# Two graph-attention layers and a mixture of experts on one core: attention on all context rows, its result gathered onto x by accumulating DMAs

## What is computed

```python
def gat_layer(x, adj, W, a_self, a_neigh, b):
    feat = jnp.einsum('nf,hfo->hno', x, W)
    e = leaky_relu(attn_self[:, :, None] + attn_neigh[:, None, :])
    e = e + MASK_VAL * (1.0 - adj)[None, :, :]
    alpha = jax.nn.softmax(e, axis=-1)
    out = jnp.einsum('hnm,hmo->hno', alpha, feat) + b[:, None, :]
    return jax.nn.elu(out reshaped to [n, 512])

h = gat_layer(ctx, a, W0, ...);  attn = gat_layer(h, a, W1, ...)   # ctx [4,512,128], a = layernorm(x)
x = x + attn                                                      # x [4,512,512]
x = x + moe(layernorm(x))       # 32 experts, top 4 of 3 groups, capacity 80, and a shared expert
```

## Time and profile before

| | |
|---|---|
| Timed runs | 534.85 us median (534.33 to 535.29) |
| Span of the profiled execution | 546.9 us, 6487 instructions |
| The profiled execution's own time | not listed beside the timed runs; only its span is known |
| PE busy (matmul) | 445.7 us, 81% |
| PE weight load | 341.5 us, 62% |
| DVE | 290.4 us, 53% |
| ACT | 158.5 us, 29% |
| POOL | 125.7 us, 23% |
| DMA | 85.56 MB, 156 GB/s over the span |

### The profile page before, as it was taken

The page is one execution under the profiler, slowest core; times in us unless marked ns, Lnnn a source line. Parts: engine busy times, 40 slices in busy tenths (PEclk is TensorE's granted clock), DMA queues, the critical chain, the costliest instruction groups (busy, mean ns, idle before and its releaser), DMA issues.

```text
span 546.9 us, 6487 instructions
## 1 busy us (share of the span) xinstructions
PE 445.7 (81%) x2363; PEld 341.5 (62%) x2363; DVE 290.4 (53%) x718; ACT 158.5 (29%) x274; POOL 125.7 (23%) x118
## 2 busy tenths in 40 slices
PE   0241687889968888997999999999999999999920
PEld 0220343333454566875789898888887888888810
DVE  5853638868975999867142254332444344343300
ACT  0222422333277301110122142333324233233320
POOL 0477200200000100000130343432132334233211
PEclk9997679889978999998985999999999999999985
DMA  9597060100126500000068967899979797987251
GB/s 259 149 198 184 24 231 0 77 38 40 78 78 232 194 10 11 0 2 0 15 136 240 274 209 252 241 291 280 292 218 340 214 295 200 333 248 238 36 89 12
DMA packets 41058, 85.56 MB, mean 156 GB/s; under 512 B 14496, under 2 KB 14496, under 8 KB 39488
## 3 DMA queue, kind: packets, MB, share of 16 engines
q1 hardware_dynamic: 32208, 67.74, 37.1%
q0 software_dynamic: 6720, 16.07, 15.1%
q10 hardware_dynamic: 2096, 1.31, 0.8%
HBM read 67.01 MB, written 18.10 MB: 156 GB/s over the span
## 4 chain that ended last, share of the span: by engine, by line
PE 55%; DVE 16%; DMA 15%; issue 6%; ACT 3%; POOL 2%; another core or an unknown queue 1%; ACTq 0%; POOLq 0%; DVEq 0%
PE bank L1268 16%; PE bank L1158 9%; PE bank L1160 9%; PE bank L1159 9%; DMA out_dram<-ctx_buf,tok 8%; PE bank L1216 7%; DMA out_dram<-room 3%; PE bank L1153 3%; DVE bn L847 2%; DMA room<-rows_dram,tok 1%; PE bank L1199 1%; DMA ix<-idx_dram,ixg 1%; DVE xs L906 1%; DMA xs<-in_x_dram 1%; DVE e1r L905 1%
## 5 line engine op out<-in xcount | busy, mean ns | idle before, releaser
L1268 PE MATMUL bank<-e1r,ring 128*128 128x80 f32 x1024 | 126.1, 284 | 1.1 <-issue 1.1
L1268 PEld LDWEIGHTS bank<-e1r,ring 128*128 128x128 f32 x1024 | 124.9, 202 | 1.3 <-issue 1.2
L654 POOL DMA_INDIRECT out_dram<-ctx_buf,tok x32 | 50.4, 1576 | 156.2 <-DMA out_dram<-ctx_buf,tok 74.4
L1076 DVE SCALAR_TENSOR_TENSOR sg<-th,bank 128x160 f32<-128x160 f32 (+1 forms) x48 | 21.3, 443 | 120.5 <-ACT th L785 96.0
L785 ACT ACTIVATE th<-bank 128x160 f32<-128x160 f32 (+1 forms) x48 | 19.3, 402 | 164.3 <-PE bank L1160 82.2
L1216 PE MATMUL bank<-w,h1T 128*128 128x512 f32 x128 | 62.0, 644 | 5.4 <-DVE sg L900 3.4
L1084 DVE TENSOR_TENSOR down<-ring,down 128x1024 fp32r<-128x1024 f32 x32 | 39.2, 1225 | 45.9 <-ACT down L762 45.0
L624 POOL DMA_INDIRECT room<-rows_dram,tok x32 | 30.3, 946 | 94.2 <-ACT tok L672 84.7
L1216 PEld LDWEIGHTS bank<-w,h1T 128*128 128x128 f32 x128 | 26.0, 207 | 39.6 <-issue 31.8
L762 ACT ACTIVATE down<-ring 128x1024 fp32r<-128x1024 f32 x32 | 33.8, 1057 | 32.6 <-PE bank L1160 32.6
L1153 PE MATMUL bank<-ident,ring 128*128 128x128 f32 x48 | 8.5, 337 | 27.9 <-DMA ring<-n_L_ffn_shared_gate_dram 13.4
(11 more groups left out here) (171 smaller groups left out, 753.9 us busy)
## 6 DMA issues: line engine op xcount, KB each, us to landing
ring<-in_L_ffn_W_gate_dram SPq DMA_DIRECT2D x32, 512.0 KB
ring<-in_L_ffn_W_up_dram SPq DMA_DIRECT2D x32, 512.0 KB
ring<-in_L_ffn_W_down_dram SPq DMA_DIRECT2D x32, 512.0 KB
xs<-in_x_dram SPq DMA_DIRECT2D x4, 1024.0 KB, 6.1
out_dram<-xs SPq DMA_DIRECT2D x4, 1024.0 KB, 3.9
out_dram<-room POOLq DMA_DIRECT2D x4, 1024.0 KB, 7.9
rows_dram<-ctx_buf SPq DMA_DIRECT2D x2, 1024.0 KB, 5.4
rows_dram<-h1T SPq DMA_DIRECT2D x2, 1024.0 KB, 4.9
```

Of the source, the lines that this page charges most:

```text
L654: pool.indirect_dma_start(out=out_rows, out_offset=bass.IndirectOffsetOnAxis(ap=tok[:, n:n + 1], axis=0), in_=ey[:, n % 3, :], in_offset=N ...
L1076: link(v.scalar_tensor_tensor(sg[:, i % 2, 0:cols], h, 1.0, bank[2 + i % 2][:, 0:cols], ALU.add, ALU.mult))
L1268: last = pe.matmul(bank[2 + i % 2][:, at:at + CAP], w[:, c, P * k:P * k + P], xgT[:, e % 3, c, :], start=(c == 0), stop=(c == KC - 1))
```

## The change

The first layer runs on the context rows in the order in which they are loaded, and so does the second. Its result z (ELU plus one) goes to DRAM, one tensor per graph, one store per tile (`store_z`). POOL gathers row i(i(n)) of z onto row n of `xs` with an indirect DMA that adds (`gather_z`), four per graph. The one too many is in every element alike, which a layer norm doesn't see, and is taken away where the shared expert's output is copied (`bias=minus_one`). The order is written anew: `before_choice` holds graphs 0 and 1, then all engines read the flag (`choose`), and `after_choice` holds graphs 2 and 3. The weights' groups are spread between the products of the second layer. The flag is worked out earlier and from sums of squares on ACT (`squares_of`) in place of DVE's statistics; its limit rises from 40000 to 150000 and is compared in another form. W1 is loaded by ACT with 1 KB in a piece where it was 256 B. Since z's ring stands in the slots of `ring`, no expert's weights are loaded before z is stored.

```diff
-        att_order = ["W0", "T0", "A0", "W1", "T1", "V0", "A1", "S0", "B0", "T2", "A2", "B1", "T3", "A3", "B2", "B3", "W2", "R0"]
+        before_choice = ["T0", "A0", "T1", "A1", "Z0", "Z1", "Z2", "Z3", "S", "Z4", "W00", "Z5", "W01", "Z6", "F", "Z7"]
+        after_choice = ["T2", "W02", "A2", "W03", "T3", "W10", "A3", "W11", "Z8", "W12", "Z9", "W13", "Z10", "W20",
+                        "Z11", "W21", "Z12", "W22", "Z13", "W23", "Z14", "R", "Z15"]
...
         @block.sync
+            def store_z(n):
+                g, t = n // TPG, n % TPG
+                sp.wait_ge(e_ready, n + 1)
+                sp.dma_start(z_dram[g].rearrange("(p t) d -> p t d", p=P)[:, t, :],
+                             zb(n)).then_inc(z_stored[n % ZRING], 16)
...
+            for g in range(GRAPHS):
+                sp.dma_start(ctx_all[:, g, :, :], ctx_in[g].rearrange("(p t) f -> p t f", p=P)).then_inc(ld_ctx[g], 16)
+                if g == 0:
+                    load_x(0)
+            for g in range(1, GRAPHS):
+                load_x(g)
...
+            def first_rows(store):
+                for g in range(2):
+                    for n in range(TPG * (g + 2), TPG * (g + 3)):
+                        store(n)
+                    sp.wait_ge(x1_ready[g], 16 * TPG)
+                    store_x1(g, x1_stored[g])
...
-            for e in range(RING - 1):
-                sp.wait_ge(tp_full, G_STEP[f"W{e}"] + KC)
-                load_gate_up(e)
-                load_down(e)
-            for g in range(GRAPHS - 1):
-                sp.wait_ge(x1_ready, TPG * (g + 1))
-                store_x1(g, x1_stored[g])
-            sp.wait_ge(x1_ready, TILES)
-            unless_one_hot(sp, slow_sync)
-            for g in range(GRAPHS):
+            def store_rows(g):
                 sp.wait_ge(xn_ready, TPG * (g + 1))
                 sp.dma_start(rows_dram[SEQ * g:SEQ * g + SEQ, 0:D].rearrange("(p t) d -> p t d", p=P),
                              xn[g % 2][:, :, :]).then_inc(rows_x[g % 2], 16)
-                if g == 1:
-                    store_x1(GRAPHS - 1, x1_stored[GRAPHS - 1])
-            sp.wait_ge(tp_full, G_STEP[f"W{RING - 1}"] + KC)
-            load_gate_up(RING - 1)
-            load_down(RING - 1)
+
+            store_rows(0)
+            for g in range(2, GRAPHS):
+                sp.wait_ge(x1_ready[g], 16 * TPG)
+                store_x1(g, x1_stored[g])
+            for i in range(ZRING):
+                sp.wait_ge(z_stored[i], 16 * ((TILES - 1 - i) // ZRING + 1))
+            for e in range(RING):
+                sp.wait_ge(tp_full, W_LAST[e] + 1)
+                load_gate_up(e)
+                load_down(e)
+            for g in range(1, GRAPHS):
+                store_rows(g)
...
         @block.gpsimd
+            def gather_z(g):
+                for n in range(TPG * g, TPG * g + TPG):
+                    pool.wait_ge(z_stored[n % ZRING], 16 * (n // ZRING + 1))
+                pool.wait_ge(idxg_ready, g + 1)
+                pool.wait_ge(squares, TPG * g + TPG)
+                for t in range(TPG * g, TPG * g + TPG):
                     pool.indirect_dma_start(
+                        out=xs[:, t, :], out_offset=None, in_=z_dram[g],
+                        in_offset=bass.IndirectOffsetOnAxis(ap=ix2[:, t:t + 1], axis=0),
+                        compute_op=ALU.add).then_inc(x1_ready[g], 16)
...
+                gather_z(0)
+                gather_z(1)
+                gather_idx2(2)
+                gather_idx2(3)
+                for g in range(2, GRAPHS):
+                    pool.wait_ge(idx2_ready[g], 16 * TPG)
+            pool.wait_ge(consts, 5)
+            power(0)
+            power(1)
+            gather_z(2)
+            power(2)
+            gather_z(3)
+            power(3)
...
         @block.scalar
+            act.dma_start(w1[:, :, :, :], W1.rearrange("h (p c) o -> p h c o", c=KC)).then_inc(ld_w1, 16)
+            def squares_of(t):
+                act.wait_ge(ld_x[t // TPG], 16)
+                if t >= 2:
+                    act.wait_ge(squares, t - 1)
+                act.activation(squared[:, t % 2, :], xs[:, t, :], ACT.Square, accum_out=ssq[:, t:t + 1]).then_inc(squares, 1)
...
         @block.vector
             def second(n):
                 v.wait_ge(ez_ready, n + 1)
-                link(v.scalar_tensor_tensor(e1[:, n % 2, :], th[:, n % 2, :], 1.0, sg[:, n % 2, :], ALU.min, ALU.max))
-                v.scalar_tensor_tensor(xs[:, n, :], e1[:, n % 2, :], -1.0, xs[:, n, :], ALU.add,
-                                       ALU.add).then_inc(x1_ready, 1)
+                if n >= ZRING:
+                    v.wait_ge(z_stored[n % ZRING], 16 * (n // ZRING))
+                v.scalar_tensor_tensor(zb(n), th[:, n % 2, :], 1.0, sg[:, n % 2, :], ALU.min, ALU.max).then_inc(e_ready, 1)
...
+            first(0)
+            for n in range(2 * TPG):
+                if n == 6:
+                    for g in range(2, GRAPHS):
+                        largest_ctx(g)
+                    smallest_gap()
+                    decide_weights()
+                if n + 1 < 2 * TPG:
+                    first(n + 1)
...
+            decide()
+            choose(v, slow_vector)
...
+            row_stats(0)
+            variances(0)
+            first(2 * TPG)
+            for n in range(2 * TPG, TILES):
+                if n + 1 < TILES:
+                    first(n + 1)
+                if n == 8:
+                    low_weight("W12")
+                    scales(0)
...
+            for g in range(2, GRAPHS):
+                row_stats(g)
+                variances(g)
+                scales(g)
```

More of the change, by code:

```diff
@@ new lines, in bounds @@
+            def bounds():
+                pe.wait_ge(worst_ready, 2)
+                for c in range(4):
+                    pe.transpose(bank[4][0:1, P * c:P * c + P], worst[:, c:c + 1], ident[:, :])
+                pe.matmul(bank[3][:, 0:2 * KC], ones[:, :], prod[:, :, :], start=True, stop=True).then_inc(worst_full, 1)
+            pe.wait_ge(consts, 2)
+            for step in before_choice:
+                if step == "S":
+                    magnitudes()
+                elif step == "F":
+                    bounds()
+                else:
+                    attention(step)
```

563 lines of the change are left out of this document (283 added, 280 removed).

## The result

| kernel, timed beside each other | median, us | lowest to highest | executions |
|---|---|---|---|
| before | 534.59 | 531.26 to 535.29 | 4 |
| after | 550.36 | 547.81 to 553.67 | 4 |

The ratio is 1.032 with a 95% interval of 1.026 to 1.038: the change makes the kernel slower, by 15.8 us. The prediction had 544.7 us, slower by 9.9. The profiled execution of after took 548.03 us with a span of 546.2.

A forecast was written before the change was run, and what follows sets the result against it. The prediction took the kernel to be bound by the chain of waits up to routing, followed by a constant. From 534.85 us, less 9.9 in the attention, plus 19.8 from last row to routing, it said 544.7 us, range 532 to 555.

The forecast's parts named there:

- The constant: From DVE's routing start onward: unchanged work, so the time is the routing start plus a constant, 365.7 us.
- The pauses: ACT's pauses at 44.10 and 53.90 us: absent from timed runs, which are 12.2 us shorter, with routing at 169.1.
- Rival 2: ACT's pauses belong to every run of before, so the changed kernel ends 2.3 us sooner: 532.5 us; chance 0.12.
- The attention: From the start to DVE's last `second`: ends at 133.3 us where before had 143.2, a gain of 9.9.
- The gathers: Four accumulating gathers per graph, after z is stored: 9.5 us for four, graph 3's landed at 148.9 us.
- The row store behind the loads: Ahead of graph 3's normalization: graph 1's row store queues behind SP's loads, 6.8 MB in all, and lands at 170 us.
- Rival 1: The row store doesn't queue behind the loads: normalization at 161.4, routing at 169.8, 535.5 us, no change; chance 0.1.
- From there to routing: From graph 3's first normalization to routing: 8.4 us as before plus 0.5 for cold PE, routing at 179 us.
- That alone would be hidden: Graph 3's statistics, power and scales: ready at 154 us, hidden because normalization in before began at 160.7.

The follow-up runs named there:

- before_third: The kernel before, unaltered, profiled once more on another chip: 530.97 us.
- before_again: The kernel before, unaltered, profiled again: 544.66 us, with a median of 546.8 us over 19 executions on that chip.
- before_contig: The kernel before with its four small loads in pieces of 16 bytes instead of 4: 544.39 us median, ratio 1.002.
- plain: The changed kernel with the second layer's gathers overwriting x instead of adding to it: 548.36 us in the profiled execution.
- rows1: The changed kernel with graph 1's row store issued before the wait on graph 3's gathers: 543.63 us median, ratio to before 1.003.
- rows1_low: rows1 plus DVE taking the low halves of graphs 0 and 1 ahead of graph 3's statistics: 537.07 us median.
- rows1_low_power: rows1_low plus POOL issuing graph 3's gathers ahead of graph 2's power: 537.58 us median, ratio to before 0.987.
- all4: rows1_low_power plus ACT taking the second layer's weights' magnitudes right after graph 1's first layer: 524.49 us median, ratio to before 0.967.

## Why the prediction was right, and where it was 5.6 us short

**The constant.** Right to a few microseconds. The start of routing and 363 to 368 us make the span in all kernels, before and after. That the time of an execution is the span, as the prediction put it, is off by 1.8 us.

**The pauses.** Right where it counted. The assumption was that the timed executions lack them and that the clean kernel before has its routing at 169.1. before_third has it at 166.0 with 531.0 us; by the same rest 534.85 us goes with 169.8. That 546.9 less 12.2 came so near the median was in part luck: with the 1.8 us it is 536.5, and in before_third routing lies 15.3 us ahead of the trace that was shown, not 12.2. Rival 2, that the pauses belong to every execution, is refuted by before_third. But what it would have needed is common: on two of the chips the kernel before took 546 and 547 us, and the traces from both chips (before_again, before_contig) have the pauses. Had the first comparison come from there, the change would have come out at +0.5%. A chance of 0.12 for that was too low, with one trace in hand and it with pauses.

**The attention.** Right nearly to the microsecond for the changed kernel: the flag passed at 82.99 (82.8), the last `second` at 133.8 (133.3), POOL's power(0) at 110.55 (110). Errors cancelled inside. The first product came at 7.92, not at 9.3, which gave nothing, since the second layer then waited for its weights until 21.4. S took 8.7 us and not 5.5, since TensorE had gone to the low clock in the wait ahead of it: 2.6 us late at 50.06. This was not hidden: Z6 ended at 63.8 where the prediction had 61.8, and DVE's chain follows it directly. But the three stretches behind were each counted too long: Z4 took 5.95 us (6.3), DVE from Z6 to F 7.3 (8.2), F and Z7 6.3 (7.6). That the flag came out within 0.2 us is luck. The gain is another matter. The prediction had 9.9 us, from a last row of before at 143.2; in before_third that row ends at 139.3, so it is 5.5 us in that trace. The four timed executions of before took up to 4 us more than before_third, and no trace shows when they had that row.

**The gathers.** The mechanism was right, and the size is the step that failed. I took 0.95 us an issue and the low half of the landings and had 9.5 us for four; measured 11.7, with 1.55 us an issue, the price of the earlier trace rows that I had seen and did not take. It comes in twice: graph 2's rows landed at 139.0 (135), so graph 3's gathers started at 143.4 (139.4), and they landed at 155.1 (148.9). That is 6.2 us. The experiment plain shows that it is the adding that costs 0.6 us an issue and 1.1 us a landing.

**The row store behind the loads.** Right in kind and size. Rival 1, that the engines serve store and loads side by side, is out: it had the store landed 4.4 to 6.3 us after its issue, and it took 13.2, behind nine loads that landed one after another. The store was issued at 161.25 behind the nine loads and landed at 174.45, 19.3 us after graph 3's rows, where the prediction had 21.1. With the gathers' 6.2 that is 174.45 instead of 170. rows1 issued the store at 139.67, ahead of them all, and the wait for it was gone. The prediction cites the Trainium skill here (DMA: Bandwidth & Descriptors, "Queues, rings and completion order"), by which each DMA engine takes the descriptors of one ring in order; that section does not promise that transfers complete in order, so "cannot overtake" went further than it. The trace agrees with the order: the store landed 13.2 us after its issue behind the loads, where a store of the same size took 4.4.

**From there to routing.** 8.4 us, as before; the half microsecond for a cold TensorE was not needed, though its granted clock was 0.51 from 174 to 183 us, where before had 1.00 (172 to 181). Sum of the routing's start: 179 + 6.2 - 1.8 - 0.5 = 182.9, 3.9 later than predicted. What follows in the profiled execution is 363.3 and 1.8 us, 0.6 less than the 365.7 that the prediction used, and the median lies 2.3 above that execution: 3.9 - 0.6 + 2.3 = 5.6.

**What I missed.** "That alone would be hidden", said of graph 3's scales. It would not. In after DVE's low halves of graphs 0 and 1 stand behind graph 3's scales, and TensorE's banks behind those; that wait alone holds the routing at 176.7. Rival 1, without the queue, was therefore not 535.5 us: rows1 has the store out of the way, as that rival would. Only with the low halves moved as well (rows1_low) does the normalization of graph 3 start at 161.95 and the routing at 170.3, where the rival had 161.4 and 169.8. So the 19.8 us between last row and routing, which the prediction charges to gathers and queue, have a third cause. After's routing lies 16.9 us behind that of before_third; moving the store takes back 6 us of that and moving the low halves as well another 6. What moving the low halves alone would bring wasn't run; by the trace of after the store would still be waited for until 174.45.

**Faster or slower.** The change does shorten the attention: the last row ends at 133.8, in before_third at 139.3. It loses more behind it, 49.1 us to the routing against 26.7. Where the kernel before pauses, its attention ends later still (155.4 in the trace that was shown), and the two are nearly even.

## What to carry to other kernels

A transfer that is moved behind a late wait on a queue's issuing engine takes all that stands behind it along; look which stores are waited for and issue them first. Where one wait is removed, look for the next that ends within a few microseconds, here DVE's order of work, before the gain is counted. A small piece of work that TensorE waits for in the middle of a full stretch costs its wait and the clock behind it: five activations moved by some 15 us brought 11 to 12 us, more than the whole change had gained in the attention.

## What the runs showed of the hardware

- An accumulating gather of 128 rows of 2 KB into SBUF took POOL 1.55 us and landed after 6.0 us (medians of 16, after); without adding 0.95 and 4.9 (plain). Issued together with two 1 MB stores of SP, four of them landed after 9.3 to 9.8 us each (rows1_low_power).
- Nine loads of 512 KB and a store of 1 MB, all issued by SP within 6 us, landed in the order of their issue, about 1.3 us for each 512 KB (after).
- TensorE idle for 6.1 us at 35 to 41 us had a granted clock of 0.67 in 5 of them (36 to 41) and 0.50 in the 8 us behind; without the wait 32 one-column products took 3.75 us and not 6.83 (after, all4).
- The kernel before took 531 to 535 us in three comparisons and 546 to 547 in two. In the traces of the slower kind ACT stood still for 11 to 14 us between 42 and 58 us, though its inputs were ready and the views name no releaser but "issue" and "remote", an unknown one; in those of the other kind it did not. Two of the 19 executions beside before_again took 534.3 and 536.6 us, so whether it goes by chip or by execution isn't settled; no trace shows those two. It isn't the 4-byte pieces. SP issued its small loads at the same place 0.5 us apart where there was no pause and 1.4 us apart where there was one. They are hardly the only cause, since plain has two shorter pauses of this mark without them; whether they play a part stays open, as the kernels that held them back never ran on a chip that pauses. The loading of code is out: in the three traces with long pauses no DMA of the instruction queues ran between 29 and 68 us. GpSimd was issuing gathers during most of these pauses, in plain too, but it did so as well in before_third, which has none.
